# Cross-attention and a quantised feed-forward layer on one core: 28 transposed blocks of X taken from TensorE and turned by transposing transfers

## The reference

```python
def _layernorm(x, eps=1e-05):            # over the last axis
    return (x - mean(x)) / sqrt(var(x) + eps)

def xattn(up, down, Wq, Wk, Wv, Wskip):  # up: (b, 128, 1024), down: (b, 128, 256)
    q, k, v = Wq @ up, Wk @ down, Wv @ down
    attention = softmax(q.T @ k / sqrt(128), axis=-1)     # (b, 1024, 256)
    return Wskip @ up + v @ attention.T

def ffn(x, gate, up, down):              # int4 weights, scale and zero per group of 64
    Wg, Wu, Wd = dequantize(gate), dequantize(up), dequantize(down)
    return (silu(x @ Wg.T) * (x @ Wu.T)) @ Wd.T           # 1024 -> 2752 -> 1024

x = x + xattn(_layernorm(x), ctx, Wq, Wk, Wv, Wskip)
x = x + ffn(_layernorm(x), gate, up, down)
```

## Time and profile before

| | before |
|---|---|
| median of 3 executions | 1394.29 us |
| the profiled execution's own time | 1394.08 us |
| its span, first to last instruction | 1392.3 us |
| PE busy | 1379.8 us, 99% |
| DVE busy | 1114.7 us, 80% |
| ACT busy | 689.5 us, 50% |
| POOL busy | 310.1 us, 22% |
| feed-forward products begin | 196.65 us |
| granted TensorE clock | 0.999 of full |

### The profile page before, as it was taken

How to read it: one execution, slowest core, us unless ns; L and a number is a source line. 1 busy time by engine, 2 the same in 40 slices (tenths; PEclk the granted TensorE clock), 3 DMA queues, 4 the chain that set the end, 5 groups by cost and what they waited for, 6 DMA issues and landing times.

```text
span 1392.3 us, 19584 instructions
## 1 busy us (share of the span) xinstructions
PE 1379.8 (99%) x6414; PEld 676.7 (49%) x6414; DVE 1114.7 (80%) x1599; ACT 689.5 (50%) x1284; POOL 310.1 (22%) x364
## 2 busy tenths in 40 slices
PE   8999999999999999999999999999999999999998
PEld 6777764444444444444444444444444444444443
DVE  6898989987887877877878778788788788788466
ACT  7999984444344344444444444444444444434440
POOL 1133323122122122122222222222222212212200
PEclk9999999999999999999999999999999999999999
DMA  6222222477477486476576666756846746748797
GB/s 193 103 103 102 78 82 61 93 129 134 96 138 133 86 158 121 98 138 126 105 139 113 110 134 114 128 113 114 147 95 127 124 106 120 133 96 151 120 278 284
DMA packets 58982, 174.83 MB, mean 126 GB/s; under 512 B 8000, under 2 KB 11072, under 8 KB 54592
## 3 DMA queue, kind: packets, MB, share of 16 engines
q0 software_dynamic: 34560, 83.90, 39.0%
q1 hardware_dynamic: 24096, 90.20, 20.9%
q10 hardware_dynamic: 288, 0.26, 0.1%
HBM read 73.67 MB, written 100.66 MB: 125 GB/s over the span
## 4 chain that ended last, share of the span: by engine, by line
PE 96%; ACT 2%; DVE 1%; issue 1%; DMA 0%; DVEq 0%; POOL 0%; POOLq 0%; SPq 0%
PE ps L592 54%; PE ps L630 9%; PE ps L632 9%; PE ps L631 9%; PE ps L555 3%; PE ps L526 3%; PE ps L802 2%; PE ps L514 2%; PE ps L550 2%; PE ps L754 1%; PE ps L545 1%; ACT temps L879 1%; PE ps L502 0%; PE ps L504 0%; ACT temps L853 0%
## 5 line engine op out<-in xcount | busy, mean ns | idle before, releaser
L592 PE MATMUL ps<-xt,w_gu 128*128 128x512 f16 x3528 | 795.6, 379 | 0.7 <-DVE temps L1573 0.7
L592 PEld LDWEIGHTS ps<-xt,w_gu 128*128 128x128 f16 x3528 | 345.1, 98 | 416.6 <-DVE temps L1573 1.1
L996 ACT ACTIVATE stage<-ps,pow 128x512 f32<-128x512 f32 x300 | 204.2, 686 | 316.7 <-PE ps L632 315.0
L1608 DVE SCALAR_TENSOR_TENSOR stage<-ps,pow,stage 128x512 f32<-128x512 f32 x220 | 160.0, 746 | 101.8 <-ACT stage L996 63.5
L630 PE MATMUL ps<-park 128*128 128x512 f16 x560 | 212.2, 379 | 0.9 <-issue 0.9
L631 PE MATMUL ps<-park 128*128 128x512 f16 x560 | 212.2, 379 | 0.0
L632 PE MATMUL ps<-park 128*128 128x512 f16 x560 | 212.2, 379 | 0.0
L439 POOL DMA_DIRECT2D out<-stage x80 | 70.5, 882 | 434.8 <-DVE stage L1608 434.8
L453 POOL DMA_DIRECT2D out<-stage x80 | 69.0, 863 | 297.6 <-ACT stage L996 297.4
L993 ACT CAST park<-temps 128x512 f16<-128x512 f32 x140 | 83.1, 614 | 67.8 <-DVE temps L1592 35.4
L1605 DVE TENSOR_TENSOR park<-temps,park 128x512 bf16<-128x512 f32 x140 | 97.8, 705 | 16.1 <-ACT park L993 13.3
(11 more groups left out here) (141 smaller groups left out, 1621.3 us busy)
## 6 DMA issues: line engine op xcount, KB each, us to landing
out<-stage POOLq DMA_DIRECT2D x80, 512.0 KB, 5.3
out<-stage POOLq DMA_DIRECT2D x140, 256.0 KB, 5.4
grid<-grids SPq DMA_DIRECT2D x136, 256.0 KB, 6.2
raw<-packed SPq DMA_DIRECT2D x34, 512.0 KB, 4.3
out<-stage SPq DMA_DIRECT2D x16, 512.0 KB, 2.8
stage<-x SPq DMA_DIRECT2D x12, 512.0 KB, 3.6
xt<-out SPq DMA_DIRECT2D x12, 512.0 KB, 12.1
out<-xt SPq DMA_DIRECT2D x12, 512.0 KB, 3.2
```

The source lines that it names most:

```text
L592: mm = pe.matmul(bank, w_gu[e][:, wp, w, P * j:P * j + P], xt[:, xb, xp, j, cols], start=(fresh and n == 0), stop=(n == 3 * J - 1), skip_g ...
L996: return act.activation(dst, ps[:, bank, :], ACT.Copy, scale=pow2[:, 10:11])
L1608: return dve.scalar_tensor_tensor(out=part, in0=ps[:, bank, :], scalar=pow2[:, 10:11], in1=part, op0=ALU.mult, op1=ALU.add)
```

## The change

The blocks and sums of the first seven pairs are no longer transposed by PE, except those of the last pair (now four entries in `LATE`). ACT, DVE and POOL read the block as it lies in `xn2` (every second column of a row), form high and low part, untransposed, in one of four staging places (`SLOTS`, used in turn), and SP issues one transposing transfer of 256 KB for each of the operands, which writes both parts into `xt`: 45 in the order `TURNED`, and four more (`TURNED_LATE`) with staging places of their own. The copy of X12 falls away, since the sums read X12 in `xn2`. A staging place is written again when the transfer four before has landed (`staging_free`). To make room the keys `kk` and half of the transposed probabilities `prob_t` move into columns of `xt` that are filled last. In the first instance `LATE` has lost its first entry, so each remaining block stands one product earlier on PE; DVE's list keeps its order.

```diff
-LATE = [(LAST - 1, X21), (LAST, X12), (LAST, X22), (LAST, X11), (LAST, X21)]
+LATE = [(LAST, X12), (LAST, X22), (LAST, X11), (LAST, X21)]
+TURNED = [u for i in range(STEPS) for part in turned_in_step(i) for u in part]
+TURNED_LATE = [(LAST - 1, X21), (LAST - 1, T1), (LAST - 1, T2), (LAST - 1, T4)]
+SLOTS = 4
...
+        slots = [space.bitcast(F16).rearrange("p (a j r) -> p a j r", a=2, j=J)
+                 for space in (temps[:, 2, 0, :], temps[:, 2, 1, :], spare[:, 1536:2048], more[:, :])]
+        kk = [last_columns[:, X22, J * s:J * s + J, :] for s in range(2)]
...
+            def turn(units):
+                for k, u in units:
...
+                    if u in (X11, X21, X22):
+                        sp.wait_ge(s_block_lo, NTH_BLOCK[k, u] + 1)
+                    else:
+                        sp.wait_ge(s_sum_lo, nth_sum(k, u) + 1)
...
+                    sp.dma_start(xt[:, u, :, :, P * k:P * k + P].rearrange("p a j t -> p (a j) t"),
+                                 src.rearrange("p a j r -> p (a j) r"), transpose=True).then_inc(done, 16)
...
             for i in range(B):
+                if i >= 4:
+                    turn_begin(i - 3)
                 load_batch(i)
...
                 if i >= 4:
+                    turn_end(i - 3)
                     store_batch(i - 4)
...
                 if i != 1:
                     energies(i, 0)
-                if block_of_step(i, "between"):
-                    block_transposed(block_of_step(i, "between"))
...
-                if block_of_step(i, "after"):
-                    block_transposed(block_of_step(i, "after"))
...
             def last_step(at):
                 if at == 0:
-                    block_transposed(block_of_step(B, "between"))
                     values(B - 1, 0)
                 if at == 1:
                     probs_transposed(B - 1, 1)
-                    block_transposed(block_of_step(B, "after"))
                     values(B - 1, 1)
                 if 2 <= at < 6:
                     block_transposed(LATE[at - 2])
-            def last_block(at):
-                if at == 0:
-                    block_transposed(LATE[4])
...
+            def staging_free(k, u):
+                if (k, u) in TURNED_LATE:
+                    act.wait_ge(s_att, 2 * B - 2)
+                else:
+                    n = NTH_TURNED[k, u]
+                    wait(act, s_turned[n % SLOTS], 16 * (n // SLOTS))
+            def row_hi(k, u):
+                act.wait_ge(s_xn2, 2 * k + 1 + int(u == X22))
+                staging_free(k, u)
+                act.copy(staged(k, u, 0), row_part(k, u).rearrange("p (j r) -> p j r", j=J)).then_inc(s_block_hi, 1)
...
                 if block_of_step(i, "between"):
-                    block_hi(block_of_step(i, "between"))
+                    row_hi(*block_of_step(i, "between"))
...
 # DVE's list first_instances
                 normalize(1, B - 1)
-                block_done(LATE[0])
+                block_done((LAST - 1, X21))
...
                 c22_out(0)
-                block_done(LATE[2])
+                block_done(LATE[1])
                 first_sums(4, 4)
                 c21_out(0)
                 second_sums(4, 0)
-                block_done(LATE[3])
+                block_done(LATE[2])
```

More of the change, by code:

```diff
@@ L66 @@
 XNS2 = 4
[L67 to L70 removed]
+LATE = [(LAST, X12), (LAST, X22), (LAST, X11), (LAST, X21)]
+NTH_LATE = {u: n for n, u in enumerate(LATE)}
+NTH_SPLIT = {u: n for n, u in enumerate(LATE[1:])}
 SUMS = [T3, T1, T2, T4]
@@ L76, in nth_sum, with first_sum_of_step, second_sum_of_step, turned_in_step @@
     return 4 * k + SUMS.index(u)
+def first_sum_of_step(i):
+    k = (i - 5) // 2
+    return [(k, T1 if i % 2 else T4)] if k >= 0 else []
+def second_sum_of_step(i):
+    k = (i - 5) // 2 if i % 2 else (i - 4) // 2
+    return [(k, T2 if i % 2 else T3)] if k >= 0 else []
+def turned_in_step(i):
+    blocks = [block_of_step(i, w) for w in ("between", "after")]
+    between, after = ([u] if u and u[1] != X12 else [] for u in blocks)
+    return between + first_sum_of_step(i), after, second_sum_of_step(i)
+TURNED = [u for i in range(STEPS) for part in turned_in_step(i) for u in part]
+NTH_TURNED = {u: n for n, u in enumerate(TURNED)}
+TURNED_LATE = [(LAST - 1, X21), (LAST - 1, T1), (LAST - 1, T2), (LAST - 1, T4)]
+NTH_BLOCK = {u: n for n, u in enumerate(u for u in TURNED + TURNED_LATE if u[1] in (X11, X21, X22))}
+SLOTS = 4
+MORE_SLOT = 3
+def slot_uses(slot, units):
+    return sum(n % SLOTS == slot for n in range(units))
 def uses_of_step(i):
-    between, after = (block_of_step(i, w) for w in ("between", "after"))
-    uses = [("block", between)] if between else []
+    uses = []
     if i >= 1:
@@ L145, in build, with row_part @@
         x12 = more[:, :].rearrange("p (c r) -> p c r", c=8)
+        def row_part(k, u):
+            rows = xn2[:, (2 * k + int(u in (X12, X22))) % XNS2, :]
+            return rows.rearrange("p (n two) -> p two n", two=2)[:, int(u in (X21, X22)), :]
         last_columns = xt[:, :, :, :, :].rearrange("p u a j t -> p u (a j) t").bitcast(F32)[:, :, :, (GT - P) // 2:]
@@ L534, in block_transposed @@
                 pe.wait_ge(s_xn2, 2 * k + 1 + int(second))
-                if unit not in LATE:
-                    bank_free(("block", unit))
+                if u == X12:
+                    use_over(max(n for n in range(len(USES)) if n % 3 == 2))
                 elif u == X22:
-                    pe.wait_ge(s_x12, k + 1)
+                    pe.wait_ge(s_x12, 1)
                 else:
-                    pe.wait_ge(s_xt_lo, sum(n < NTH_UNIT[unit] and v[1] != X12 for n, v in enumerate(UNITS)))
-                bank = ring_bank(("block", unit))
+                    pe.wait_ge(s_xt_lo, NTH_SPLIT[unit])
+                bank = ps_m
                 for j in range(J):
```

155 lines of the change are left out of this document (98 added, 57 removed).

## The result

| | before | after |
|---|---|---|
| median (runs) | 1394.29 us (4) | 1413.72 us (4) |
| profiled execution: time, span | 1394.08, 1392.3 | 1414.78, 1413.0 |
| feed-forward products begin | 196.7 | 201.9 |
| from there to the end of the span | 1195.6 | 1211.1 |

The ratio is 1.0138 [1.0127, 1.0150]. The direction was forecast, the size was not: 1399.5 was the value, and the result lies just outside the range, which ended at 1413. The two last lines of the table, both from the profiled executions, split the 20.7 us of span: 5.2 are lost in the attention loop, where 1.2 were to be gained, and 15.5 behind it, where 6.4 were to be lost.

The account below looks back on a forecast made before the run. The prediction took PE's own queue to bound both stages, with ACT 0.3 us behind it in the loop. Its terms, -5.0 + 3.8 + 6.4 = +5.2 us, gave 1399.5 us, with a range of 1392 to 1413.

Parts of the forecast that it names:

- PE's blocks go, ACT next at 11.7 us: Attention loop: without PE's transposes ACT decides at 11.7 us a step on average, taken as -5.0 us.
- The sign that the text itself named for being wrong: Prediction is wrong if PE passes the first instance's blocks unstopped, or the loop alone becomes longer than before.
- DVE now runs three such operations (T1, T2, X11's low part, each 0.7 us as before): Loop, even steps: three DVE operations with two SBUF inputs delay POOL by 0 to 2 us, taken as 0.7.
- Places, 3.8 us: Loop: ACT waits four times for staging places, 1.3 + 1.3 + 0 + 1.2 = 3.8 us, with landing at 2.8 us.
- Slow transposing transfers as the pace of the loop: Loop: transfers occupying the queue over 3.3 us each pace it, some 100 us more at 6.2 us; chance 0.05.
- SP's turns at nothing: Loop: SP issues seven transfers in two steps, 0.33 us each; loads go out later but in time, cost nothing.
- The context loads: Loop sign: SP's context loads 11.7 us apart in undisturbed steps; 11.2 or 12.2 would say otherwise about ACT or DVE.
- The first instance, +6.4: First feed-forward instance: block waits 2.5 + 3.0 + 3.2, less 0.9 old wait and 1.4 blocks gone; 2.8 to 8.0 us.
- The two that follow from queue order alone: First instance: PE waits at X11 and X21 for low parts queued behind DVE's c22_out and c21_out, 3.0 and 3.2 us.
- No wait for staging places: Rival, loop: transfers land in 2.0 us or so and POOL is not delayed; +1.4, 1395.7 us; chance 0.21.
- slow transposing transfers: Rival, loop: landing at 5 us gives 1408 us, at 6.2 about 1413; chance 0.25, of which 0.05 paced loop.
- faster: Rival: PE near 11.3 us a step (-9), first instance +2.8, no place late; -6, 1388 us; chance 0.09.

Follow-up runs that it names:

- the first experiment: The changed kernel with the last pair's four blocks standing one product later again: 1402.03 us, 1.0059 against the kernel before.
- the third: The changed kernel with POOL computing only 16 of 512 columns of the sums' low parts in pairs 2 to 6: 1404.39 us, 1.0072 against the kernel before.

## Why the prediction was wrong

Of the 20.7 us that the span grew by, 5.2 were forecast. The other 15.5 are 6.4 in the loop and 9.1 behind it. Two steps of the prediction failed: DVE's operations were held to take what they had taken, and a wait of PE was priced at its own length.

**PE's blocks go, ACT next at 11.7 us.** Right as to PE, wrong as to who follows. "Bounds: 11.8 us (25 blocks by 0.47, ACT no limit) and 2 us (DVE takes ACT's place)" was in the text, and even that end assumed that DVE's sums stay at 0.7 us. With POOL out of their way and no wait for staging places, the loop gains 3.0 us up to the products (193.7 against 196.7), where 5.0 were forecast for it. So this term was inside its bounds but for the next point. The sign that the text itself named for being wrong, a loop that alone becomes longer than before, is what came.

**The step that failed in the loop** is "DVE now runs three such operations (T1, T2, X11's low part, each 0.7 us as before)". I costed the exclusion on POOL, 0.7 us, and wrote that it "speaks against this change on DVE too", without a price. DVE was 19.15 of 20 us busy before; 23 sums at 1315 and 1093 ns in place of 683 are 12 us more, and some low parts add to that. That is the mis-sized term: it stood at 0 in the sum, and it is worth most of the 6.4 us between forecast and trace at the products' start, and 7 to 9 us in the experiments (1413.7 to 1404.4 and 1402.0 to 1394.6), in which the staging places gain a little too. The rows for it were at hand, since the earlier trace rows show POOL held up by DVE; by symmetry the same row holds for the other order. The Trainium skill, "SBUF — State Buffer", section "SBUF: two separate sides", says that whichever of the two starts first has the port for its whole instruction and the other is blocked. The traces agree, with 1.63 us for a sum of 0.68 that began just behind an operation of 1.16.

**Places, 3.8 us.** The waits in the trace come to 3.8 us, in three pieces and not four. The number is right by luck: landing was 3.2 to 4.5 us, not 2.8, and the steps were longer. With POOL in another order the waits vanish, and with small low parts in the old order 2.7 us of them stayed; that they came from low parts queued late on POOL is the likely reading, but no run tests it alone. Slow transposing transfers as the pace of the loop (5 in 100) did not happen, and with plain ones the time is the same. The prediction's estimate of 10.5 us, eight squares in series at the 1309 ns that the Trainium skill, "VectorE: DVE Perf Modes", section "The three transpose paths", gives for one, does not hold: the median landings were 3.2 to 4.5 us.

**SP's turns at nothing.** Right in effect, though not as costed: an issue takes 1.23 us or more, not 0.33. No engine's waits between 60 and 206 us name a load of x or of the context, and with the issue at 0.60 us the time was the same. The context loads were no good clock any more: they now stand behind transfers that wait for POOL, and went out 11.6 to 14.5 us apart, not 11.7. Four of them:
```profile
114.05 0.42 SPq L375 DMA_DIRECT2D w_gu<-ctx  x1
126.76 0.45 SPq L375 DMA_DIRECT2D w_gu<-ctx  x1
138.88 0.46 SPq L375 DMA_DIRECT2D w_gu<-ctx  x1
...
153.35 0.46 SPq L375 DMA_DIRECT2D w_gu<-ctx  x1
```

**The first instance, +6.4.** The waits were forecast as 2.5, 3.0 and 3.2 us and came as 3.88, 3.15 and 3.27. The two that follow from queue order alone were right to 0.15 us. X12's was longer: I had let DVE be 1 us sooner with the last values. It was not. Its normalization ended at 219.66, 3.8 us behind PE's arrival at 215.84 (219.72 less the wait of 3.88); before it was 2.8, 214.16 against 211.40. PE alone came sooner.
```profile
218.01 1.65 DVE L1429 TENSOR_SCALAR park<-stage,mv,rstd 128x1024 f32<-128x1024 f32 x1
219.58 1.65 DVE L1479 TENSOR_TENSOR xt<-park,xt 128x512 f32<-128x512 f32 x1
```
These two are 1.65 us beside POOL, the normalization before as well. **The step that failed here** is the sum "2.5 + 3.0 + 3.2 - 0.9 - 1.4 = +6.4 us", which has no term for the clock and prices each wait at its own length. The 10.3 us of waits, 1.6 more than the 8.7 forecast, carried 5 to 7 us of slow products behind them: in the profile 7.4, the largest single part of the 15.5 us that the forecast missed. The early blocks alone made the kernel before 13.3 us slower.

**Rivals.** "No wait for staging places", "slow transposing transfers" and "faster" all failed; none of them had DVE as the bound, the mechanism that decided the loop, or the clock. The 1408 to 1413 us of the slow-transfer case came near the result by luck, for another reason.

## What to carry to other kernels

Moving an operand of a DVE operation from PSUM to SBUF changes more than its source: check what POOL runs at that time and price both orders, the second to arrive pays. If one of the two engines has time, give it a wait that makes it come second; here this alone was worth some 8 us and kept all the work. A wait on PE of around 3 us cost its length plus the slow stretch behind it in these traces, so a block moved one product earlier is not priced by its wait alone. And ask what is left when both are mended: 28 blocks off PE, 13 us of its queue at 0.47 each, ended as 2 us, since ACT and DVE were both near full (19.67 and 19.60 of 20 us in one stretch of the loop, POOL out of the way).

## What the runs showed of the hardware

- The granted clock behind a wait of PE: 0.66 to 0.73 in the next slice of 5 us behind waits of 2.65 us, 0.71 in the slice in which one of 3.15 ended, 0.50 behind 3.27 and 3.88, and 1.00 behind 2.12, and behind the loop's waits of 1.7. The length alone does not decide it: behind 2.26 us in the loop of the first experiment it was 0.73, behind 2.37 at the same place of the third it was 1.00.
- A transfer of 256 KB from SBUF to SBUF with 2-byte transposition landed in 3.2 to 4.5 us on the median, about as a plain one between the same tiles did (3.4 to 3.8, and 6.7 for the last four), but held SP for 1.23 us or more at its issue, where the plain one took 0.60.
- DVE's normalization, with one large SBUF input, and POOL's two-input operation held each other up as well: 1.67 us for POOL's in place of 1.16 where DVE was first, 1.20 for DVE's in place of 0.81 where POOL was (and 1.65 in the first instance).
